# Four-layer graph network: the order of adjacency tiles in the last stage, and of the group closings in layers 2 to 4

## The reference, cut to what matters

```python
# block 2, for each of 4 layers
hw = h @ Ws[l]
agg = jnp.zeros_like(hw).at[dst].add(enorm * hw[src])
agg = agg + self_norm * hw + bs[l]
mean = jnp.mean(agg); var = jnp.mean(jnp.square(agg - mean))
h = jax.nn.relu(ln_w[l] * (agg - mean) * jax.lax.rsqrt(var + EPS) + ln_b[l])
# block 3
cat_feat = jnp.concatenate([h_x[dst], h_e, h_mu[dst]], axis=1)
agg = relu(jax.ops.segment_sum(cat_feat, src, num_segments=N) @ W4.T)
x = x + relu(h_x + h_mu + agg)
# block 4: sums, maxima and means of edge_attr over src, then two dense layers
```

## Time and profile before

| | |
|---|---|
| median of 3 runs | 13834.2 us (13832.89 to 13850.3) |
| the profiled execution | 13845.09 us |
| its span, first to last instruction | 13843.3 us |
| busy share of the span: PE / DVE / ACT / POOL | 52% / 52% / 35% / 39% |
| layers 2 to 4 | from 10846 to 12836 us of the span |
| last stage's matmuls | from 12938 to 13829 us |
| mean granted TensorE clock | 0.697 of 2.4 GHz over the span; 0.93 in the last stage |

### The profile page before, as it was taken

The page is one execution under the profiler, slowest core; times in us unless marked ns, Lnnn a source line. Parts: engine busy times, 40 slices in busy tenths (PEclk is TensorE's granted clock), DMA queues, the critical chain, the costliest instruction groups (busy, mean ns, idle before and its releaser), DMA issues. The chain is left out here.

```text
span 13843.3 us, 151624 instructions
## 1 busy us (share of the span) xinstructions
PE 7164.9 (52%) x44130; PEld 5810.4 (42%) x44130; DVE 7167.8 (52%) x18509; ACT 4855.9 (35%) x7954; POOL 5410.8 (39%) x5426
## 2 busy tenths in 40 slices
PE   2333333325555555550053000036399999999788
PEld 2222222214454444440032000035255788888676
DVE  5556555634444444442042000158378777777666
ACT  0000000003333333330042000014288777777566
POOL 4555555555555555555714777720300000000111
PEclk6555555556666666665576555568699999999899
DMA  3334333423222222227185000039366888888798
GB/s 125 121 121 133 127 121 120 137 80 66 64 65 63 64 65 63 65 57 40 29 219 147 20 20 20 3 84 223 76 204 204 240 272 254 274 253 271 158 186 173
DMA packets 2774800, 1739.57 MB, mean 126 GB/s; under 512 B 1804710, under 2 KB 2613388, under 8 KB 2773940
## 3 DMA queue, kind: packets, MB, share of 16 engines
q1 hardware_dynamic: 2434740, 1298.35, 36.7%
q10 hardware_dynamic: 165920, 277.72, 5.6%
q0 software_dynamic: 173408, 154.46, 5.0%
HBM read 1065.70 MB, written 506.69 MB: 114 GB/s over the span
## 5 line engine op out<-in xcount | busy, mean ns | idle before, releaser
L838 POOL DMA_INDIRECT records<-RT,IDX x1664 | 1620.3, 974 | 1470.2 <-ACT RT L1598 972.1
L808 POOL DMA_INDIRECT G<-node_table,IDX x1664 | 1605.3, 965 | 1351.7 <-issue 1286.0
L882 POOL DMA_INDIRECT adj<-OH,EA x1664 | 1720.2, 1034 | 639.3 <-issue 639.3
L1276 PE MATMUL PS<-ring_f,terms_r 128*128 128x448 f32 x8232 | 1725.0, 369 | 34.3 <-DVE ring_f L2525 24.9
L1276 PEld LDWEIGHTS PS<-ring_f,terms_r 128*128 128x128 f32 x8232 | 1531.7, 188 | 216.7 <-DVE ring_f L2525 68.5
L2525 DVE CAST ring_f<-raw_f 128x1792 fp32r<-128x1792 uint8 x1323 | 1409.3, 1092 | 395.3 <-DMA raw_f<-adj 245.2
L1762 ACT CAST ring_f<-raw_f 128x1792 fp32r<-128x1792 uint8 x882 | 1465.5, 1691 | 418.4 <-DMA raw_f<-adj 260.3
L1052 PE MATMUL PS<-OH 128*98 128x128 bf16 x3328 | 453.5, 317 | 1806.9 <-remote 855.4
L1052 PEld LDWEIGHTS PS<-OH 128*98 128x98 bf16 x3328 | 365.8, 199 | 1973.4 <-remote 884.3
L2037 DVE TENSOR_TENSOR_SCAN S<-M,S,PS 128x512 f32<-128x512 bf16 x621 | 791.8, 1275 | 748.8 <-issue 517.1
L2030 DVE TENSOR_SCALAR OH<-iota_b,AG 128x128 bf16<-128x128 bf16 (+1 forms) x4480 | 836.0, 269 | 567.5 <-issue 290.6
(11 more groups left out here) (404 smaller groups left out, 14295.4 us busy)
## 6 DMA issues: line engine op xcount, KB each, us to landing
raw_f<-adj SPq DMA_DIRECT2D x2205, 224.0 KB
adj<-Z ACTq DMA_DIRECT2D x105, 1568.0 KB
AG<-adj SPq DMA_DIRECT2D x735, 224.0 KB
G<-records SPq DMA_DIRECT2D x624, 128.0 KB
M<-same_dst SPq DMA_DIRECT2D x416, 128.0 KB
fill_rows<-Z ACTq DMA_DIRECT2D x104, 512.0 KB
runs_l<-R SPq DMA_DIRECT2D x208, 256.0 KB
G<-fill_rows SPq DMA_DIRECT2D x208, 256.0 KB
```

Source lines behind the costliest of these rows:

```text
L808: pool.indirect_dma_start(G[:, i, q * D:(q + 1) * D], None, table, bass.IndirectOffsetOnAxis(ap=IDX[:, i, q:q + 1], axis=0)).then_inc(sem( ...
L838: pool.indirect_dma_start(rec, bass.IndirectOffsetOnAxis(ap=IDX[:, i, q:q + 1], axis=0), RT[:, i, q, :], None).then_inc(sem(f"scattered{i} ...
L882: pool.indirect_dma_start(adj_cells, bass.IndirectOffsetOnAxis(ap=CELL[:, at:at + 1], axis=0), VAL[:, at:at + 1], None).then_inc(sem(f"cel ...
L1276: m = pe.matmul(half_of(x, h)[:, c, :], stat, RINGF[q % NR][:, h * QW + c * HW:h * QW + (c + 1) * HW], start=K == 0, stop=False, skip_grou ...
```

## The change

In the last stage the order of the tiles in a group is no longer bytes first, one-hots last. `ORDER[g]` places one one-hot tile after every 14 byte tiles in groups 1 to 6 (positions 14, 29, 44, 59, 74, 89, 104), and in group 0, where the list of rows is ready only late, after every fifth byte tile from 68 on (positions 68, 74, ... 104). Byte tile K goes to ACT if K is even, otherwise to DVE; the one-hots stay with DVE. The places of `finish`, `gather3`, `store3`, `mlp` and `turned` now go by the position in the group. `evacuate` is split: ACT copies half 0, DVE half 1 (semaphore `group_used`), both at position 3 of the next group, where it was position 4 before; PE waits for both. In layers 2 to 4 the closing is spread over 30 tiles: DVE joins after tile 12 and 19, scales after 25, takes statistics after 30; ACT copies one half after tile 7 and one after 14. SP's instructions keep their order.

```diff
+        def order(g):
+            spread = [NJ * (k + 1) // NV if g else NJ - NR * (NV - 1 - k) for k in range(NV)]
+            rows = []
+            for K in range(NJ):
+                rows.append(K)
+                rows += [NJ + k for k in range(NV) if spread[k] == K + 1]
+            return rows
...
-        ON_ACT = [K < NJ and n % 2 == 0 for n, (_, K) in enumerate(TILE)]
+        TILE = [(g + 1, K) for g in range(NJ // (2 * GT)) for K in ORDER[g]]
+        ON_ACT = [K < NJ and K % 2 == 0 for _, K in TILE]
...
-            def shift(l, g):
+            def shift(l, g, h):
                 act.wait_ge(sem("group_done"), l * NG2 + g + 1)
-                act.wait_ge(sem("joined"), l * (2 * NG2) + (2 * g + 4 - 2 * NG2))
-                for h in range(2):
-                    act.copy(split_cols(SHIFT[h * D:(h + 1) * D, :]), half_of(g % 2, h)[(1 - h) * D:(2 - h) * D]).then_inc(sem("shifts"), 1)
+                act.wait_ge(sem("joined"), l * (2 * NG2) + (2 * g + h + 3 - 2 * NG2))
+                act.copy(split_cols(SHIFT[h * D:(h + 1) * D, :]), half_of(g % 2, h)[(1 - h) * D:(2 - h) * D]).then_inc(sem("shifts"), 1)
...
-                    to_f32r(it + g * GI, 0, NR)
-                    shift(l, g - 1)
-                    to_f32r(it + g * GI, NR, STEP)
+                    for h in range(2):
+                        to_f32r(it + g * GI, h * 7, (h + 1) * 7)
+                        shift(l, g - 1, h)
+                    to_f32r(it + g * GI, 14, STEP)
...
-                    to_f32r(it + g * GI, 0, NR)
+                    to_f32r(it + g * GI, 0, 12)
                     join(l, g - 1, 0)
-                    to_f32r(it + g * GI, NR, NR + 2)
+                    to_f32r(it + g * GI, 12, 19)
                     join(l, g - 1, 1)
-                    to_f32r(it + g * GI, NR + 2, NR + 4)
+                    to_f32r(it + g * GI, 19, 25)
                     scale_r(l, g - 1)
-                    to_f32r(it + g * GI, NR + 4, NR + 6)
+                    to_f32r(it + g * GI, 25, 30)
                     stats_r(l, g - 1)
-                    to_f32r(it + g * GI, NR + 6, STEP)
+                    to_f32r(it + g * GI, 30, STEP)
...
-                for h in range(2):
-                    t = act.copy(split_cols(EV[:, h * QW:(h + 1) * QW]), half_of(0, h))
-                t.then_inc(sem("zl_ready"), 1)
+                act.copy(split_cols(EV[:, 0:QW]), half_of(0, 0)).then_inc(sem("zl_ready"), 1)
...
+            def evacuate(g):
+                dve.wait_ge(sem("ring_free"), RE + NR + (g + 1) * AB)
+                if g:
+                    dve.wait_ge(sem("xl"), NG2 + g)
+                dve.tensor_copy(split_cols(EV[:, QW:2 * QW]), half_of(0, 1)).then_inc(sem("group_used"), 1)
```

More of the change, by code:

```diff
@@ L259, in gnn_kernel @@
         VIRT_AT = LAST_OF[NJ // (2 * GT) * (NCK - 1) - 1] // NR
-        TILE = [(g + 1, K) for g in range(NJ // (2 * GT)) for K in range(NJ + NV)]
+        def order(g):
[5 more added lines that the diff above has]
+            return rows
+        ORDER = [order(g) for g in range(NJ // (2 * GT))]
+        assert all(sorted(rows) == list(range(NJ + NV)) for rows in ORDER)
+        TILE = [(g + 1, K) for g in range(NJ // (2 * GT)) for K in ORDER[g]]
         FIRST = {t: n for n, t in enumerate(TILE)}
-        ON_ACT = [K < NJ and n % 2 == 0 for n, (_, K) in enumerate(TILE)]
+        ON_ACT = [K < NJ and K % 2 == 0 for _, K in TILE]
         RE = UE * AB
@@ L1431, in turned @@
                 pe.wait_ge(sem("zl_ready"), (LAYERS + 2) * NG2 + g + 1)
+                pe.wait_ge(sem("group_used"), LAYERS * NG2 + 3 + g)
                 for b in range(GT):
@@ L1445, in _ @@
             for g in range(NG2):
-                for K in range(NJ + NV):
+                for p, K in enumerate(ORDER[g]):
                     n = FIRST[g + 1, K]
-                    r = K // NR
-                    if K % NR == 0:
+                    r = p // NR
+                    if p % NR == 0:
                         if r == 2 and g:
@@ L1456, in _ @@
                     made(n)
-                    if g and K == 0:
+                    if g and p == 0:
                         pe.wait_ge(sem("zl_ready"), (LAYERS + 2) * NG2 + g)
+                        pe.wait_ge(sem("group_used"), LAYERS * NG2 + 2 + g)
                     if g == 0 and K == NJ:
@@ L1464, in _ @@
                             m = pe.matmul(half_of(0, h)[:, c, :], stat, RINGF[n % NR][:, h * QW + c * HW:h * QW + (c + 1) * HW],
-                                          start=K == 0, stop=K == NJ + NV - 1, skip_group_check=True)
+                                          start=p == 0, stop=p == AB - 1, skip_group_check=True)
                     m.then_inc(sem("ring_free"), 1)
@@ L1865, in evacuate @@
             def evacuate(g):
[L1867 removed]
+                act.wait_ge(sem("ring_free"), RE + NR + (g + 1) * AB)
                 if g:
                     act.wait_ge(sem("xl"), NG2 + g)
[L1870 to L1872 removed]
+                act.copy(split_cols(EV[:, 0:QW]), half_of(0, 0)).then_inc(sem("zl_ready"), 1)
             def virtual_e():
@@ L1886, in _ @@
                     act.copy(RINGF[n % NR][:, :], raw[:, 0:2 * QW, K % 2]).then_inc(sem("conv_a"), 1)
[L1887 to L1890, removed]
+                p = n % AB
+                r = p // NR
+                if p == NR - 2 and g >= 2:
+                    evacuate(g - 2)
+                if p % NR == NR - 1:
                     if g == 1 and r == 6:
@@ L2736, in _ @@
                                           bc(srj[:, (K - NJ) * 2 * GT:(K - NJ + 1) * 2 * GT], [P, 2 * GT, P]), ALU.is_equal).then_inc(sem("conv_d"), 1)
-                r = K // NR
-                if K % NR == NR - 1:
+                p = n % AB
+                r = p // NR
+                if p == NR - 2 and g >= 2:
+                    evacuate(g - 2)
+                if p % NR == NR - 1:
                     if g >= 2 and r < 5:
@@ L2749, in _ @@
                             store3((g - 1) * 2 + m)
+            evacuate(NG2 - 1)
             for k in range(3, 5):
```

3 lines of the change are left out of this document (2 added, 1 removed).

## The result

| | before | changed |
|---|---|---|
| median | 13836.76 us (4 runs, 13832.89 to 13850.3) | 13752.01 us (4 runs, 13744.07 to 13775.83) |
| ratio | | 0.994, 95% interval 0.9922 to 0.9957 |
| profiled execution | 13845.09 us | 13775.83 us |

The changed kernel is faster by 84.8 us, 0.6%. The forecast was 111.6 us less, to 13722 us; the measured time lies inside the range, 30 us above the likeliest value.

A forecast was written before the change was run, and what follows sets the result against it. Last stage bound in turns by DMA (bytes) and DVE (one-hots), layers 2 to 4 by PE; gains 69.6 (groups 1 to 6) + 11 (group 0) + 1 (copies) + 30 (closings) = 111.6 us, giving 13722 us, range 13680 to 13785.

The forecast's parts named there:

- The floor of 108.3 us: Last stage: a group's 49 pairs at 2.21 us are 108.3 us of DMA, which covers the one-hots on average.
- The closings: Layers 2 to 4: spreading them takes away 1.7 us at each of 18 boundaries, 30 us (12 to 38).
- each 1.09 us of DVE finds enough time to spare: Layers 2 to 4: each spread closing piece finds 1.15, 1.0 and 0.8 us to spare, so PE should hardly stop.
- One-hots that meet `finish` or `gather3`: Groups 1 to 6: lateness of 2.2 us at position 14, 2.0 at 24 to 29, 1.0 at 74.
- Lone one-hots: Groups 1 to 6: four of seven one-hots meet no other work and cost 0.1 to 0.3 us in sum.
- the boundary: Between last-stage groups: PE stops 1.1 us plus a wait for tiles; five ring slots cover most, taken as 0.7 us.
- Group 0: First group of the last stage: of some 16 us, 11 gained (5 to 15) by one-hots from position 68 on.
- My signs: Expected: DMA share over 1.0 throughout, copies 114 us apart, PE's one-hot waits near zero, clock 1.00 behind a boundary.
- the 2.3 at which I had called myself wrong: Last stage: the prediction is wrong if the seven-pair stretches slow below 2.3 us for a pair.
- The closings give nothing: Rival, 7%: in layers 2 to 4 the plain DMAs are late at the boundary, so the stop only moves; 13752 us.
- Lateness in full: Rival, 19%: three buffers' round trip sets the last stage's pace, each DVE delay shifts later pairs; groups 119, total 13755 us.
- The slower case: Rival, 3%: in the last stage a one-hot empties all three buffers, each restart costs 4 to 5 us; 13900 us.

The follow-up runs named there:

- thin casts: Changed kernel with last-stage casts over 448 of 1,792 columns and one-hots over 256 (wrong sums): 10045.11 us against 10211.0 for the kernel before, one run.
- the best version: Changed kernel with a fourth raw pair buffer, copies placed earlier and one-hots moved away from `finish` and `gather3`: 13693.18 us, ratio 0.9887 to the kernel before.
- the order alone: Kernel before with only the new last-stage tile order, closings as before, both group-sum copies on ACT where they were: 10178.01 us, ratio 0.9968.
- early copies and other places: Changed kernel with copies behind byte tiles 0 and 1 and one-hots of groups 1 to 6 moved from `finish` and `gather3`: 13752.26 us, ratio 0.9921.
- early copies: Changed kernel with ACT's copy behind byte tile 0 and DVE's behind byte tile 1, instead of 2 and 3: 10101.43 us, ratio 0.9895 to the kernel before.
- the fourth buffer: Changed kernel with a fourth raw buffer for last-stage pairs: 10052.69 us, ratio 0.9851 to the kernel before; with copies placed earlier too, 10051.49 us, 0.9847.
- the repeated run: The changed kernel again, unaltered, beside the kernel before: 13775.7 us against 13864.53, ratio 0.9939, 118.1 us a group.

## Why the prediction was right, and where it was off

**The floor of 108.3 us held.** Counting casts in stretches without one-hots gave 2.21 us for a pair; thin casts gave 107.9 us a group, the best version 107.5. What lies behind the number, transfers or their issuing on SP, stays open. The Trainium skill's figure for a transposing DMA with a non-contiguous middle dimension (DMA: Bandwidth & Descriptors, section Latency and other measured facts, 261 GB/s) would have put the floor near 86 us, an estimate from that page; no run came near it, and the highest rate over a group was 220 GB/s, with all of its traffic counted.

**The closings held**: 28.0 us where 30 was forecast, and 32 in the run with them alone. PE runs through the boundary, and the one group shown takes 87.7 us where I had put 88.5. My step that each 1.09 us of DVE finds enough time to spare between its casts is what the trace shows.

**One-hots that meet `finish` or `gather3`: about right.** Forecast 5.2 us a group; moving them away gave 4.3, thinning them 4.4. **Lone one-hots: right**, since the two runs leave next to nothing for them.

**The step that failed is the boundary**, "five ring slots cover most of it. I take 0.7". I had counted PE's stop as 1.1 us plus a small wait and taken the ring to cover it. The stop was 3.2 us, because ACT's copy stood behind two casts that had waited for pairs; PE then ran at half its clock for about 3 us, where I had expected 1.00 behind a boundary; and in the changed kernel the whole was paid about in full. Halving the stop gave 1.4 us; the order alone, with 6.1 us, cost 3.0 more. With PE stopped and then slow, casts wait, and the raw buffers behind them stay taken; the trace has the waits and a DMA share of 0.01 behind them, but that one leads to the other is read from their order in time. By the same ratio the 3.2 us cost about 3, an estimate, against 0.7. That holds for casts of full length; with thin casts the same stop cost nothing that can be seen, and why is open. How much of the 3 is the stop and how much the clock, no run takes apart.

So 118.2 is 107.9, plus 4.3 for the meetings, plus about 3 for the boundary, and 3 that no run takes apart. With early copies and other places 112.8 is left, of which the remaining stop is 1.3. The rest is presumably the parts of `finish` and `gather3` by themselves, which delay casts as one-hots do; I had counted them as part of the 2.21. This is only argued. That it is lateness is shown, since the fourth buffer takes it: with early copies it leaves 108.3.

**Group 0**: 5.1 instead of 11 (7.9 in the repeated run). One-hots, `store3` and `gather3` crowd from position 64 to 80 there. I had seen that and set it too low; no run tested it apart.

**My signs.** The DMA share was above 1.0 in the mean of a whole group, though not throughout, and the waits before one-hots nearly vanished, as I had said. The copies came 118.2 us apart, not 114; a pair took 2.31 us in the stretch shown, just past the 2.3 at which I had called myself wrong; and the clock behind the boundary failed, as told.

**The rivals.** Two of them came nearer to the 13752 in numbers than my 13722. *The closings give nothing* had named 13752 itself; that is chance, since the closings gave 28 us and the groups fell short instead. *Lateness in full* (a group at 119, total 13755) was close in its group as well, 118.2. But its reason, three buffers as the pace, is refuted by the thin casts: the floor is there without any lateness of the casts, and lateness costs on top of it, as far as the buffers don't take it. That the forecast put such lateness halfway between paid and absorbed was the softer part of the sum; for the meetings it was nearly right, for the boundary not. The slower case (a one-hot empties all buffers) did not occur. That the total lies inside my range says little for the sum: the range was wide enough for both rivals.

## What to carry to other kernels

Where two engines or queues bound a stage in turns, mixing their work gains up to the shorter turn, but only as far as the buffers between them reach: here the order and the copies brought 8 of 18 us a group, and one more buffer 8 of the rest. Once the transfers set the pace, ask of each stop behind them whether it keeps a buffer from coming back: here PE's stop cost about its own length with full casts, with three buffers and with four, and nothing that could be seen with thin casts. Place an instruction that others wait for ahead of one that waits for data, and look at the clock behind a stop, not only at the stop. A spread that is even by count is not even in time: put added work where that engine has nothing else.

## What the runs showed of the hardware

At best the transposing DMAs delivered a pair of 448 KB in 2.19 to 2.21 us over whole groups, 208 to 209 GB/s, with three issued ahead (thin casts, 107.9 us for 49 pairs) or four (108.3 and 107.5), at DMA shares of 1.2: a fourth issued ahead did not raise this rate. SP's instruction that issues one lasted 1.2 to 4.5 us in these runs, 1.97 and 2.01 in the median of the two shown.

The granted TensorE clock was 0.50, the 1.2 GHz level, for some 3 us behind stops of PE of 3.1 to 3.9 us in the changed kernel, and 1.00 behind stops of 1.3 us with early copies and other places.

The part of the kernel ahead of layer 2, in which POOL issues nearly 5,000 indirect DMAs, took 10846 to 10889 us in the first profiles and in two series of runs, and 7203 to 7212 us in the other two, with the same code. The stages behind it were not visibly touched by it: the last stage, the same in the kernel before (long part) and with the closings alone (short part), took 126.1 and 126.0 us a group, and the layers with the new closings 1954 to 1963 and 1948 to 1959 us. What sets it stays open: it went by the series, not by the kernel. A total is therefore compared only with that of the kernel before beside it.
